# Attention plus feed-forward on one core: the next batch's transposes moved from TensorE to VectorE and DMA, and feed-forward matmuls placed behind each burst

## The reference

```python
xn = _layernorm(x)                       # over the last axis
# attention: q = k = v = xn, split into 16 heads
w = einsum('bhqd,bhkd->bhqk', q, k) / sqrt(16)
w = softmax(where(causal, w, min))
attn = einsum('bhqk,bhkd->bhqd', w, v)
# feed-forward, with a per-batch low-rank term made of rows 1 to 16 of xn
m1, m2 = outer products of even and odd rows of xn[:, 1:17]
h = gelu(xn @ (W1 + scale * m1).T + b1)
ffn = h @ (W2 + scale * m2).T + b2
out = x + attn + ffn
```

## Time and profile before

| | |
|---|---|
| time, median of 3 runs (lowest to highest) | 894.2 us (893.68 to 894.57) |
| the profiled execution: time, span | 894.16 us, 892.4 us |
| busy: PE | 833.6 us (93%) |
| busy: ACT | 686.0 us (77%) |
| busy: DVE | 662.3 us (74%) |
| busy: POOL | 256.7 us (29%) |
| chain that ended last: PE, ACT, DVE, DMA | 86%, 8%, 3%, 2% |
| granted TensorE clock, mean | 0.997 |

### The profile page before, as it was taken

How to read it: one execution, slowest core, us unless ns; L and a number is a source line. 1 busy time by engine, 2 the same in 40 slices (tenths; PEclk the granted TensorE clock), 3 DMA queues, 4 the chain that set the end, 5 groups by cost and what they waited for, 6 DMA issues and landing times.

```text
span 892.4 us, 16213 instructions
## 1 busy us (share of the span) xinstructions
PE 833.6 (93%) x6272; PEld 431.7 (48%) x6272; DVE 662.3 (74%) x1356; ACT 686.0 (77%) x737; POOL 256.7 (29%) x520
## 2 busy tenths in 40 slices
PE   1579999999999999999999999999999999999997
PEld 1154644545454554545545464454545445454543
DVE  7787698867978579775997679786797868973242
ACT  0458788887887878888788878888788787888874
POOL 1213233131432314233241324313143231412211
PEclk9999999999999999999999999999999999999999
DMA  4967437391665816465173834739165561712202
...
DMA packets 187053, 110.22 MB, mean 124 GB/s; under 512 B 138785, under 2 KB 155233, under 8 KB 185953
## 3 DMA queue, kind: packets, MB, share of 16 engines
q1 hardware_dynamic: 186976, 109.18, 51.3%
...
## 4 chain that ended last, share of the span: by engine, by line
PE 86%; ACT 8%; DVE 3%; DMA 2%; SPq 1%; issue 0%; DVEq 0%
PE o_ps L437 26%; PE work L465 22%; PE work L452 20%; PE scores L417 16%; ACT probs L370 4%; ACT L370 2%; PE work L479 1%; ACT gelu L384 1%; DMA even<-even_dram 1%; DMA xn<-x 1%; DVE w_lo L582 1%; DVE xt_w L615 1%; DMA q_dram<-xt_pair 1%; DVE w L600 0%; DVE w_hi L579 0%
## 5 line engine op out<-in xcount | busy, mean ns | idle before, releaser
L370 ACT ACTIVATE probs<-scores 128x1024 f32<-128x1024 f32 x576 | 556.7, 1024 | 145.0 <-PE scores L417 144.8
L362 POOL TENSOR_SCALAR_AFFINE_SELECT probs<-probs 128x256 f32<-128x256 f32 x512 | 254.1, 518 | 624.3 <-ACT probs L370 621.6
L437 PE MATMUL o_ps<-probs,v_ones 128*32 128x512 f32 (+3 forms) x3072 | 279.4, 493 | 0.0
L417 PE MATMUL scores<-q_stack,k_stack 64*128 64x512 f16 (+3 forms) x1536 | 181.8, 330 | 34.3 <-ACT probs L370 22.8
L437 PEld LDWEIGHTS o_ps<-probs,v_ones 128*32 128x32 f32 x3072 | 83.9, 109 | 136.6 <-issue 126.7
L417 PEld LDWEIGHTS scores<-q_stack,k_stack 64*128 64x128 f16 x1536 | 53.4, 94 | 189.1 <-ACT probs L370 136.1
L452 PE MATMUL work<-xt_hi,w_hi 128*128 128x512 f32 x256 | 104.1, 407 | 3.6 <-DVE gelu L659 3.6
L465 PE MATMUL work<-g_hi,w_hi 128*128 128x512 f32 x256 | 106.0, 414 | 0.0
L465 PE MATMUL work<-g_lo,w_hi 128*128 128x512 f32 x256 | 105.0, 410 | 0.0
L465 PE MATMUL work<-g_hi,w_lo 128*128 128x512 f32 x256 | 103.8, 406 | 0.0
L452 PE MATMUL work<-xt_hi,w_lo 128*128 128x512 f32 x256 | 100.4, 392 | 0.0
...
## 6 DMA issues: line engine op xcount, KB each, us to landing
q_dram<-xt_pair SPq DMA_DIRECT2D x32, 512.0 KB, 4.6
...
k_stack<-k_dram SPq DMA_DIRECT2D x128, 128.0 KB, 4.0
xn<-x SPq DMA_DIRECT2D x16, 512.0 KB, 5.1
...
k_dram<-xt_pair SPq DMA_DIRECT2D x16, 512.0 KB, 3.6
...
```

What stands on the lines that cost most here:

```text
L362: pool.affine_select(out=blk, in_=blk, compare_op=ALU.is_ge, fill=0.0, base=0, pattern=[[0, 2], [1, P]], channel_multiplier=-1).then_inc(m ...
L370: act.activation(probs[:, slot % RING, 2 * half:2 * half + 2, :].rearrange("p h q -> p (h q)"), scores[:, half, :], ACT.Exp, scale=EXP_SCA ...
L417: last = pe.matmul(scores[:, half, h * BANK + at:h * BANK + at + n], k_stack[rows, g % 2, half, kb * P:(kb + 1) * P], q_stack[rows, g % 2, ...
L437: last = pe.matmul(o_ps[VW * j:VW * (j + 1), half, q0 % BANK:q0 % BANK + n], v_ones[:, kb, heads_of(g).start + 2 * j, :], probs[:, slot % ...
```

## The change

- For batches 1 to 7, xn is no longer transposed by TensorE. In pairs 4 and 6 VectorE turns half of xn each in blocks of 32x32 (`turn_xn`, two instructions), SP stores the half to `xt_dram`, and sixteen loads of 64 KB (`load_xt`) put the blocks in order in `xt`. `split_pair` follows in pairs 8 and 9. Batch 0 keeps TensorE's transposes.
- Six passes of ffn2 stand between the value products and the second scores of pairs 2 and 11 (`BETWEEN`), the pairs after the bursts. The remaining passes are spread six to a pair. `ffn2` waits for the split of each hidden tile as it comes to it, not for all eight.
- The burst of the second token half also has its first tile a pair ahead, behind pair 9, so both bursts have seven tiles in pairs 1 and 10. `EARLY` is four for both.
- In batch 0 the first burst comes behind pair 2 with all eight tiles, and everything to pair 9 is a pair later.
- In the opening x comes in quarters, and ScalarE's queue issues part of the loads (two quarters of x, the constants, the accumulator), one of the stores of queries, and half of the first stack loads. ScalarE makes the copies `copy_v` of batch 0. `add_m2` and the splits of W2 move into pairs 0 to 2.
- `load_acc` comes after the stack loads of pair 13, and both `add_b2` in pair 17. The buffer `o_norm` is gone; `evac_o` works in place.

```diff
+BETWEEN = {
+    2: [("ffn2", 0, 0, 0, 6)],
+    11: [("ffn2", 1, 0, 0, 6)],
+}
 BEHIND = {
...
-    9: [("ffn2", 0, 1, 19, 24), ("xn", 3)],
-    10: [("ffn1", 1, 0, MT)],
+    8: [("ffn2", 0, 1, 18, 24)],
+    9: [("ffn1", 1, 0, 1)],
+    10: [("ffn1", 1, 1, MT)],
...
-FIRST = {**BEHIND, 0: [], 1: [("ffn1", 0, 0, MT)]}
-BURSTS = (1, 10)
+
+FIRST_BETWEEN = {**BETWEEN, 2: [], 3: [("ffn2", 0, 0, 0, 6)]}
...
+    2: [("ffn1", 0, 0, MT)],
+    3: [("ffn2", 0, 0, 6, 12)],
...
+def bursts(b):
+    return (1, 10) if b else (2, 10)
...
-LN_STATS, LN_RSTD, LN_APPLY, ADD_B2 = 2, 3, (3, 4), (5, 7)
+LN_STATS, LN_RSTD, LN_APPLY, TURN_XN, SPLIT_PAIR, ADD_B2 = 2, 3, (3, 4), (4, 6), (8, 9), (17, 17)
...
-EARLY = (4, 2)
+EARLY = (4, 4)
...
-        what, b, *key = piece
-        at = sum(key) % 2 if what == "ffn1" else key[1] if what == "ffn2" else key[0] % 2 if b == 0 else 0
+        at = piece[-1] % 2
...
+        xt_dram = nc.dram_tensor("xt_dram", [B, 2, P, NT // 2, DT, QUARTERS, VW], FP32, kind="Internal").ap()
...
+        xn_turned = sb("xn_turned", [P, NT // 2, DT, QUARTERS, VW])
...
+        def x_quarter(eng, b, i):
+            blocks = slice(NT // 4 * i, NT // 4 * (i + 1))
+            eng.dma_start(xn[:, blocks, :], x[b, :, :].rearrange("(t p) d -> p t d", p=P)[:, blocks, :])\
+               .then_inc(x_in[i], 16)
+
+        def acc_quarter(eng, b, j):
+            eng.dma_start(acc[VW * j:VW * (j + 1), b % 2, :, :, :],
+                          x[b, :, :].rearrange("(a r) (t j c) -> j r t a c", r=VW, t=DT, j=QUARTERS)[j]).then_inc(acc_in, 16)
+
+        def q_part(eng, b, t, part):
+            heads = slice(HEADS // DT * t, HEADS // DT * (t + 1))
+            eng.dma_start(q_dram[b, heads, :, :, part, :].rearrange("h c a s -> (h c) a s"),
+                          xt_pair[:, part, t, :].unsqueeze(1).broadcast_to([P, 2, S])).then_inc(pair_out[t], 16)
+
+        def stacks_half(eng, b, g, h):
+
+            rows = slice(HEAD_ROWS * h, HEAD_ROWS * (h + 1))
+            eng.dma_start(q_stack[rows, g % 2, :, :],
+                          q_dram[b, heads_of(g), :, :, :, :].rearrange("(u h) c a e s -> h (c a e) u s", h=2)[h])\
+               .then_inc(stacks_in[g % 2], 16)
+            for u in range(GH // 2):
+                eng.dma_start(k_stack[rows, g % 2, u, :],
+                              k_dram[b, heads_of(g), :, :, :].rearrange("(u h) c a s -> u h (c a) s", h=2)[u, h]
+                              .unsqueeze(1).broadcast_to([2 * HD, 2, S])).then_inc(stacks_in[g % 2], 16)
+
...
+            def store_turned(b, half):
+                sp.wait_ge(turned, 2 * (b - 1) + half + 1)
+                sp.dma_start(xt_dram[b, half, :, :, :, :, :].rearrange("p n t k r -> p (n t k r)"),
+                             xn_turned[:, :, :, :, :].rearrange("p n t k r -> p (n t k r)")).then_inc(turned_out, 16)
+
+            def load_xt(b, half):
+                sp.wait_ge(turned_out, 16 * (2 * (b - 1) + half + 1))
+                for t in range(DT):
+                    for k in range(QUARTERS):
+                        sp.dma_start(xt[VW * k:VW * (k + 1), t, BANK * half:BANK * (half + 1)],
+                                     xt_dram[b, half, :, :, t, k, :].rearrange("(i c) n r -> c n i r", i=QUARTERS))\
+                          .then_inc(xt_in, 16)
 
...
-            load_x(0)
-            sp.dma_start(scale_sb[:, :], scale.partition_broadcast(P)).then_inc(consts_in, 16)
-            for j in range(QUARTERS):
-                sp.dma_start(b2_sb[VW * j:VW * (j + 1), :, :],
-                             b2.rearrange("(t j c) -> j t c", t=DT, j=QUARTERS)[j].partition_broadcast(VW))\
-                  .then_inc(consts_in, 16)
-            sp.dma_start(b1_sb[:, :], b1).then_inc(b1_in, 16)
+            x_quarter(sp, 0, 0)
+            x_quarter(sp, 0, 2)
             load_w1()
-            sp.wait_ge(xn_ready, 1)
+            sp.wait_ge(xn_half_ready, 1)
             store_even(0)
-            store_heads(0, 0)
-            load_stacks(0, 0)
+            store_k(0, 0)
+            q_part(sp, 0, 0, 0)
+            sp.wait_ge(pair_out[0], 16 * STORE_DMAS)
+            stacks_half(sp, 0, 0, 0)
             load_even(0)
+            store_heads(0, 1)
             load_stacks(0, 1)
             sp.wait_ge(xt_split, 1)
             load_w2()
-            load_acc(0)
-            store_heads(0, 1)
...
-                    if b:
-                        sp.wait_ge(out_stored, 16 * OUT_DMAS * b)
-                    load_acc(b + 1)
                     sp.wait_ge(xn_ready, b + 2)
                     store_even(b + 1)
+                    store_turned(b + 1, 0)
                     sp.wait_ge(m2_added, b + 1)
                     load_even(b + 1)
                 store_acc(b, 0, 0)
+                if more:
+                    store_turned(b + 1, 1)
+                    sp.wait_ge(w2_ready, 2 * b + 2)
+                    load_xt(b + 1, 0)
+                    load_xt(b + 1, 1)
...
+                    if b:
+                        sp.wait_ge(out_stored, 16 * OUT_DMAS * b)
+                    load_acc(b + 1)
...
+            def copy_v(g):
+                act.copy(v_ones[:, :, heads_of(g), 0:HD],
+                         xn[:, :, :].rearrange("p t (h d) -> p t h d", h=HEADS)[:, :, heads_of(g), :]).then_inc(v_ready, 1)
...
+            x_quarter(act, 0, 1)
+            x_quarter(act, 0, 3)
+            act.dma_start(scale_sb[:, :], scale.partition_broadcast(P)).then_inc(consts_in, 16)
+            act.dma_start(b1_sb[:, :], b1).then_inc(b1_in, 16)
+            for j in range(QUARTERS):
+                act.dma_start(b2_sb[VW * j:VW * (j + 1), :, :],
+                              b2.rearrange("(t j c) -> j t c", t=DT, j=QUARTERS)[j].partition_broadcast(VW))\
+                   .then_inc(consts_in, 16)
+                acc_quarter(act, 0, j)
+            act.wait_ge(xn_ready, 1)
+            act.wait_ge(v_ones_made, 1)
+            copy_v(0)
+            act.wait_ge(pair_ready, 1)
+            q_part(act, 0, 0, 1)
+            copy_v(1)
+            act.wait_ge(pair_out[0], 16 * STORE_DMAS)
+            stacks_half(act, 0, 0, 1)
+            copy_v(2)
+            copy_v(3)
...
-                    pe.wait_ge(w2_ready, 2 * b + 2)
-                    pe.wait_ge(g_split, MT * (2 * b + c + 1))
+                    pe.wait_ge(w2_ready, 2 * b + 1)
...
+                    if t == 0 and n % 3 == 0:
+                        pe.wait_ge(g_split, MT * (2 * b + c) + m + 1)
+                    if t == 0 and n == FFN2_PASSES // 2:
+                        pe.wait_ge(w2_ready, 2 * b + 2)
...
+                    for what, *arg in between(b, p):
+                        ffn2(b, *arg)
                     if slot + 3 < ALL:
                         scores_of(slot + 3)
...
+            def turn_xn(half):
+                for n in range(2):
+                    blocks = slice(2 * n, 2 * n + 2)
+                    ins = dve.transpose(xn_turned[:, blocks, :, :, :].rearrange("p n t k r -> p (n t k r)"),
+                                        xn[:, NT // 2 * half + 2 * n:NT // 2 * half + 2 * n + 2, :]
+                                        .rearrange("p n d -> p (n d)"))
+                ins.then_inc(turned, 1)
             def split_pair(b, t):
-                evacuated("xn", b, 2 * t)
-                evacuated("xn", b, 2 * t + 1)
+                dve.wait_ge(xt_in, 32 * DT * QUARTERS * b)
...
-                link(dve.tensor_tensor(o_norm[:, :, :], o_t[:, :, 0:HD],
+                link(dve.tensor_tensor(o_t[:, :, 0:HD], o_t[:, :, 0:HD],
...
-            add_m2(0)
-            split_m2(0)
-            split_m2(1)
...
-                    if p not in BURSTS and not end:
-                        evac_slots()
...
+                    if b == 0 and p == 0:
+                        add_m2(0)
...
+                    if p == SPLIT_M2[1] and b or (b, p) == (0, 1):
+                        split_m2(1 if b else 0)
...
+                    if b == 0 and p == bursts(b)[0]:
+                        split_m2(1)
...
+                            dve.wait_ge(xn_ready, b + 2)
+                        for half in range(2):
+                            if p == TURN_XN[half]:
+                                if b or half:
+                                    dve.wait_ge(turned_out, 16 * (2 * b + half))
+                                turn_xn(half)
+                        if p in SPLIT_PAIR:
+                            split_pair(b + 1, SPLIT_PAIR.index(p))
+                        for t in range(DT):
+                            if p == ADD_B2[t]:
+                                add_b2(b + 1, t)
```

147 lines of the change are left out of this document (71 added, 76 removed), and 7 rows, old and new, of the table BEHIND.

## The result

The changed kernel takes **888.84 us** (median; 888.21 to 890.85) against 894.57 of the kernel before in the same comparison: ratio 0.9939, interval 0.9925 to 0.9954. It is faster, clear of the scatter of the runs, but by 5.7 us (0.6%) where 26.5 were forecast. The profiled execution has a span of 887.1 us (892.4 before) and a mean granted clock of 0.995.

A forecast was written before the change was run, and what follows sets the result against it. A floor of about 4.6 us per pair, scores and exponentials waiting for each other, was taken as the bound. Gains of 7.0 (opening), 17.5 (batches 1 to 6) and 2.0 (last), 26.5 us, took 894.2 to 867.7; range 858 to 882.

The forecast's parts named there:

- The floor of the pairs: Steady state: a pair takes at least about 4.6 us, as scores and exponentials wait for each other; six passes fit.
- Rival (b): Steady state: no floor, six-pass pairs go at their TensorE time of 4.52 us, 10 us more saved, 858; chance 0.08.
- (a): Steady state: VectorE becomes the bound; 5% slower, it costs 14.7 us over seven bursts, so 882; chance 0.2.
- Rival (c): Opening: it gives nothing, since VectorE, not the first scores, holds the burst, so 875; chance 0.1.
- 7.8 us for sixteen: Detour over DRAM: time to issue the sixteen xt loads on SP's queue, at four in 1.95 us.
- 1.5 us of cover: Detour over DRAM: xt's lateness hides with about 1.5 us to spare before TensorE would wait for a bank.
- Rival (d): Detour over DRAM: xn loads come late, sixteen taking 20.7 us to issue; 80 us of idle TensorE, 948; chance 0.05.
- moving `add_b2` at no cost: VectorE's stretch after pair 10's burst: both add_b2, 2 x 1.32 us, come in, costed at nothing with 0.2 us margin.
- the opening, 7.0 forecast: Batch 0 and before: 6.3 us gained up to pair 10 and 0.7 behind it, between 3.5 and 10.
- The first scores come 2.7 us before 30.09: Opening: issuing from two queues saves 2.05 us of stack loads and 0.7 of stores; bounds 0.6 to 4.
- VectorE is free at 50.3: Opening, first burst: VectorE is free at 50.3 instead of 50.1, and the third tile starts at 51.0 instead of 48.9.
- the 0.7 that the sum has for a slower clock: Opening, first burst: 0.7 us allowed for a slower clock, the burst ending at 60.0.

The follow-up runs named there:

- e4: Changed kernel with the ffn2 passes of w2_lo left out, four passes a pair instead of six (output incomplete): 884.03 us, a single run.
- e10: e6 with xt stored in four DMAs and loaded in one per half, a second turning buffer, even rows' load behind the detour: 868.46 us, ratio 0.9697.
- e3: Changed kernel with W2's load ahead of the second half's stores in the opening, and xt's loads ahead of store_acc: 877.85 us, ratio 0.9815.
- e6: e3 with add_b2 moved from the pair before its batch into pairs 5 and 7 of the batch: 873.89 us, ratio 0.9768.
- e1: Changed kernel with W2's load ahead of the stores of the second half's keys and queries in the opening: 883.47 us, ratio 0.9869.
- e11: e10 with the second group's stack loads behind W2's load in the opening: 868.63 us, ratio 0.9698.

## Why the prediction was wrong, point by point

Three terms of the sum failed: the loads of xt, issued at 0.70 us each instead of 0.49 and so later than the cover allowed; the move of `add_b2`, put at nothing; and the opening, where W2's landing was left out. The floor of the pairs held.

*Right: the floor, and the sum built on it.* Pairs of six passes last 4.6 us, pairs 2 and 11 6.11 (forecast 6.1), and e4's pairs of four passes, in a row, last 4.59 to 4.63. With the disturbances out of the way, e10 gains 17.5 us in batches 1 to 6, the forecast's 17.5 (its batches last 102.7 us: 245.92 - 143.23 = 102.69). Rival (b) is out, and so is (a) in the form that I gave it: VectorE's copy in pair 1 is never waited for in batches 1 to 7. Rival (c) saw that VectorE holds the opening, but expected no gain there and not a loss.

*Wrong: "7.8 us for sixteen" loads, and 1.5 us of cover.* I took the issue price from four `out<-acc` of the same shape, 0.49 us each; the loads took 0.70, 11.2 in all. The second half's store, which stands ahead of all sixteen on SP's queue, took 1.60 us to issue in batch 1 where the sum has 0.4. Instead of 15.6 us after the start of pair 6 the last load is issued at 211.06 - 191.96 = 19.1, and xt is in at 21.1 instead of 18. Of these 3.1 us over the forecast 2.05 show in pair 10 of batch 1, so the cover was 1.1 us and not 1.5. Over batches 1 to 6 that is 6.5 us, the sum of pair 10 over 12.98. Rival (d) had the mechanism, with a price far too high. The rule of the Trainium skill that stood beside it (VectorE: DVE Perf Modes, "The three transpose paths") would have made it longer than a batch, by the prediction's estimate; for runs of 128 bytes the rows after disagree: 1 MB is issued in 11.2 us and in 2 us later.

*Wrong: moving `add_b2` at no cost.* I weighed only whether VectorE would be late for TensorE. It is not; but beside its work in that place GpSimd's four masks take 2.88 us (in e3) instead of 1.68, the value product of pair 1 waits for them, and pair 1 is longer by 0.40 to 0.45 us a batch, 2.55 over batches 1 to 6 and 0.5 in the last. I had not asked which third engine works beside the moved instruction. e6 shows it: with `add_b2` elsewhere pair 1 is 12.98 again. The Trainium skill has this rule (SBUF — State Buffer, "Who interferes with whom"): an instruction of VectorE with two operands in SBUF, or a copy or cast in a fast mode, and an instruction of GpSimd that reads SBUF exclude each other for the length of an instruction. The runs agree: in e3 the masks start at 149.88, inside the additions of b2 (to 150.85), the first takes 1.25 us and all four 2.88, and the two casts of W2 that meet the later ones take 1.17 us, against 0.76 in the kernel before (at 150.72), where no mask runs beside them.

*Wrong: the opening, 7.0 forecast, -5.3 measured.* Three steps failed. (1) "The first scores come 2.7 us before 30.09": they came 0.47 before, under even the low bound of 0.6. The first stack load is issued at 21.92 instead of 22.35, and from there to the first scores it is 7.70 us against 7.74. So the half microsecond was gained ahead of the stack loads, and the second queue gave nothing, though the first group's last stack load is issued by 24.1 instead of 26.4. The DMA engines are at nine tenths or more from 24 to 46 us nearly throughout; that the bytes and not their issue set the landing would fit this, but was not shown. (2) "VectorE is free at 50.3": I counted even's load sooner, but not that W2's load now stood behind the second half's stores. W2 landed 13.6 us after its issue, VectorE was free at 56.2, and the burst lasted 68.11 - 48.17 = 19.9 us instead of 13.9. Of these 6.0 us, 3.6 are stall (5.74 against 2.1) and 2.0 are the 13 slow passes (2.7 against the 0.7 that the sum has for a slower clock, without a working). With W2 ahead of the stores e1 makes pair 2 shorter by 6.4, by order alone. (3) In batch 0 VectorE is behind and the detour is late too: pair 10 lasts 16.93 instead of the 14.06 of the kernel before; it is 14.33 in e10. Together with 1.5 us in pair 5, where VectorE's evacuation is late in every version here, and 0.1 us less up to the burst: 2.2 + 6.0 + 2.9 + 1.5 - 0.1 = 12.5, against 12.3 missing.

*The sum.* 12.3 in the opening, 6.5 + 2.6 in batches 1 to 6, less 0.2 in the last: 21.2 us, the whole difference between forecast and result. The two edits of order (e3) return 11.0 of it, `add_b2` 4.0 (most of it in pair 1; pair 2 of batch 0 is 1.2 shorter too, but pairs 1 and 10 of that batch are longer), the detour's chain 5.4. e10, another kernel than the forecast one, comes near its 867.7 with a smaller gain in the opening (5.5 instead of 7.0): what the forecast had and e10 still has not is the first scores at 27.4. Why they stay near 29.7 is open: e1, e3 and e11 took stores and other loads from behind them without effect; I did not try fewer bytes in the first stores.
